# Expert tiles and shared units of a mixture-of-experts layer, interleaved stage by stage on TensorE; the tiles' down part in three fp32r products

## The chip, the cores and the metric

One core of a Trainium2 chip runs the whole program. The metric is the device time of one execution in microseconds; for the kernel before it was taken in three runs, and one more execution was profiled. TensorE is called PE in the profile, VectorE DVE, ScalarE ACT, GpSimd POOL, and SyncE, which issues most DMAs here, SP.

## The reference

A transformer layer on 2048 tokens of width 512, all in fp32: windowed attention, residual and layer norm, then a feed-forward part with a second residual and layer norm. The feed-forward part is

```python
logits = x @ W_router.T
probs = softmax(logits)
rw, sel = top_k(probs, 2)                                  # 8 experts, 2 per token
combine = zeros((T, 8)).at[arange(T)[:, None], sel].add(rw)
sh = silu_and_mul(x @ Ws_gate_up, 1408) @ Ws_down          # shared expert
shared_out = sh * sigmoid(x @ W_sgate.T)
h = silu_and_mul(einsum('th,ehi->eti', x, We_gate_up), 352)
eo = einsum('eti,eih->eth', h, We_down)
sparse_out = einsum('eth,te->th', eo, combine)
x = layernorm(x + shared_out + sparse_out)
```

## The kernel before

The attention half is the same in both kernels and ends at about 430 us of the profile. What follows is `ffn_phase`.

Nearly every product there is made of three fp32r passes: an operand a is split into a_hi (a copy rounded to fp32r, by ScalarE) and a_lo = a - a_hi (by VectorE), and TensorE accumulates a_lo b_hi, a_hi b_lo and a_hi b_hi.

*Units.* The shared expert has 1408 hidden columns, worked off in 11 units of 128 for each of four runs of 512 tokens, 44 units in all. A unit n has a gate part, an up part and a down part, each of twelve passes of 512 columns. ScalarE applies SiLU to the gate sum, VectorE multiplies it with the up sum (`work`), both split the result into `h_hi` and `h_lo`, and the down part of unit n stands behind the gate and up parts of unit n + 1. Weights come through rings of three buffers. Gate and up sums have two PSUM banks each, the down sums four.

*Routing.* A router product, then VectorE finds the top two experts of each token, counts tokens per expert and gives each pair of token and expert a slot in 39 tiles of 128 rows. One-hot tables (`onehot_rows`, `onehot_lanes`, L1091 to L1101) and 32 small fp32 products (`index_tokens`, L1264, recorded as 64) turn this into a list of tokens per tile. The one-hot tables are made after unit 6 and TensorE uses them ahead of unit 8 (`PREFIX_AT, INDEX_AT = 4, 8`).

*Tiles.* After the first 11 units all 39 tiles follow without a unit between them. For tile i GpSimd gathers 128 rows of x; TensorE transposes them (`transpose_xe`, L1312); gate and up are 24 passes of 352 columns (`expert_gate_up`, L1322); VectorE multiplies into `e_h`; TensorE transposes h (`transpose_h`, L1338), ScalarE copies it out of PSUM; and the down part (`expert_down`, L1344) is three products in plain fp32, each recorded as two passes of 512 columns. Its result goes to DRAM (`expert_rows`). The expert's weights, 704 KB twice and 512 and 192 KB, are loaded anew for each tile; only gate and up weights are split, into the buffers that the units use, so that no unit can be under way. The tile's steps alternate between two PSUM banks of each kind.

*Combine.* Units 11 to 43 follow. Between them GpSimd gathers for each block of 128 tokens the two expert rows (`gather`), VectorE adds them with their weights (`add_rows`, two operations), adds the shared sum (`evacuate`), takes the statistics, and normalises (`normalise`), with the reciprocal root from GpSimd (`rstd_of`). This is spread over all three later runs of tokens.

The order on each engine is written out by hand as loops; each engine works its queue in that order and waits on semaphores. SP issues the loads in its own loop, each behind the wait that frees its buffer.

## Time and profile before

| | us |
|---|---|
| median of 3 runs | 1146.53 |
| lowest, highest | 1141.86, 1148.76 |
| the profiled execution | 1145.41 |
| its span, from the first to the last instruction | 1143.6 |

Share of the span that each engine was busy: PE 94%, weight loads (PEld) 75%, DVE 62%, ACT 49%, POOL 34%. The DMA queues moved 175.78 MB. A share of busy time is a mean over stages with different limits, so the rows further down go by stage. A matmul's record is longer than the distance to the next one, so distances between starts, not durations, give the pace. "issue" means that the engine waited for nothing that the profile shows.

### The profile page before, as it was taken

The numbers are of one execution on the slowest core, as the hardware profiler recorded it, in microseconds if no ns is written. First come the engines' busy times: TensorE is split into PE (matmuls) and PEld (weight loads), VectorE is DVE, ScalarE is ACT, GpSimd is POOL, SyncE is SP. The second block draws the span as 40 slices with busy tenths as digits, with TensorE's granted clock in tenths as the row PEclk, the third lists the DMA queues.
The fourth block names the chain that finished last, engine by engine and source line by source line (L and its number), as shares of the span: only waits on it lengthen the run. The fifth ranks groups of instructions, "written<-read, shape, count | busy, mean of one in ns | idle before, by whom it ended". The sixth has DMA issues, their size and how long they took to land.

```text
span 1143.6 us, 19457 instructions
## 1 busy us (share of the span) xinstructions
PE 1078.9 (94%) x7063; PEld 857.4 (75%) x7063; DVE 706.9 (62%) x1100; ACT 560.9 (49%) x1191; POOL 387.0 (34%) x529
## 2 busy tenths in 40 slices
PE   4799999999999968999999999999999999999995
PEld 3577777777777748888777777777777888878884
DVE  4697878777778741565465555565554575465465
ACT  3566666666666531332356666666663243332330
POOL 2777887687787720000001111110102221012012
PEclk8899999999999985898999999999999999999998
DMA  5102111111111005132589999999987474175132
GB/s 195 30 24 57 30 31 30 42 48 31 30 31 48 20 19 165 56 111 74 200 294 355 358 364 366 365 362 368 359 287 221 129 243 125 46 225 169 58 111 74
DMA packets 123678, 175.78 MB, mean 154 GB/s; under 512 B 10592, under 2 KB 64224, under 8 KB 123584
## 3 DMA queue, kind: packets, MB, share of 16 engines
q1 hardware_dynamic: 117904, 155.92, 41.8%
q0 software_dynamic: 5680, 18.62, 5.1%
q8 instruction: 57, 0.93, 0.4%
q14 instruction: 37, 0.30, 0.1%
HBM read 155.90 MB, written 18.61 MB: 153 GB/s over the span
## 4 chain that ended last, share of the span: by engine, by line
PE 55%; DVE 4%; DMA 1%; issue 1%; ACT 1%; SPq 0%; POOLq 0%; POOL 0%; DVEq 0%; ACTq 0%
PE down_ps L1352 9%; PE gate_ps L1292 3%; PE gate_ps L1294 3%; PE gate_ps L1293 3%; PE up_ps L1294 3%; PE up_ps L1292 3%; PE up_ps L1293 3%; PE down_ps L1308 3%; PE down_ps L1310 3%; PE down_ps L1309 3%; PE gate_ps L1333 3%; PE up_ps L1251 2%; PE gate_ps L1334 2%; PE gate_ps L1335 2%; PE up_ps L1333 2%; PE up_ps L1335 2%
## 5 line engine op out<-in xcount | busy, mean ns | idle before, releaser
L864 POOL DMA_INDIRECT rows<-x_dram,token_i x39 | 37.8, 970 | 362.0 <-PE gate_ps L1319 254.8
L1165 DVE TENSOR_TENSOR gu_lo<-e_raw,gu_hi 128x1408 fp32r<-128x1408 f32 x78 | 126.6, 1623 | 50.3 <-ACT gu_hi L935 50.0
L310 ACT ACTIVATE prob<-score_ps,nbias 128x256 f32<-128x256 f32 x256 | 119.6, 476 | 9.2 <-DVE nbias L407 8.8
L935 ACT CAST gu_hi<-e_raw 128x1408 fp32r<-128x1408 f32 x78 | 106.6, 1367 | 29.1 <-DMA e_raw<-in_We_gu 26.9
L247 POOL TENSOR_TENSOR probT<-probT,masks 128x256 f32<-128x256 f32 x128 | 97.2, 780 | 66.2 <-DVE probT L428 66.1
L1352 PE MATMUL down_ps<-ed_raw,y 128*128 128x512 f32 (+1 forms) x234 | 106.9, 593 | 0.6 <-ACT y L955 0.6
L1113 DVE TENSOR_TENSOR work<-work,up_ps 128x512 f32<-128x512 f32 x44 | 30.2, 687 | 117.3 <-PE up_ps L1294 113.1
L496 PE MATMUL proj_ps<-wqkv_lo,xT_hi 128*128 128x512 f32 x192 | 86.4, 450 | 15.7 <-DVE wqkv_lo L385 9.9
L407 DVE TENSOR_REDUCE nbias<-score_ps 128x2 f32<-128x512 f32 x128 | 88.5, 691 | 4.4
L915 ACT ACTIVATE work<-gate_ps 128x512 f32<-128x512 f32 x44 | 26.3, 598 | 120.0 <-PE gate_ps L1294 119.8
L318 ACT COPY probT<-probT_ps 128x512 f32<-128x512 f32 x64 | 37.5, 587 | 92.8 <-PE probT_ps L530 92.8
L497 PE MATMUL proj_ps<-wqkv_hi,xT_hi 128*128 128x512 f32 x192 | 78.5, 409 | 0.0
L498 PE MATMUL proj_ps<-wqkv_hi,xT_lo 128*128 128x512 f32 x192 | 78.2, 407 | 0.0
L1352 PEld LDWEIGHTS down_ps<-ed_raw,y 128*128 128x128 f32 (+1 forms) x234 | 43.3, 190 | 38.1 <-issue 37.3
L1292 PE MATMUL gate_ps<-x_hi,gu_lo 128*128 128x512 f32 x176 | 71.1, 404 | 0.4 <-DVE gu_lo L1014 0.4
L530 PE MATMUL probT_ps<-ident,prob 128*128 128x128 f32 x512 | 71.3, 283 | 0.0
L1293 PE MATMUL gate_ps<-x_lo,gu_hi 128*128 128x512 f32 x176 | 70.2, 399 | 0.0
L1294 PE MATMUL gate_ps<-x_hi,gu_hi 128*128 128x512 f32 x176 | 70.2, 399 | 0.0
L875 POOL DMA_INDIRECT rows<-expert_rows,slot_i x32 | 34.5, 1078 | 104.1 <-DVE y L1141 59.0
L1308 PE MATMUL down_ps<-wd_hi,h_lo 128*128 128x512 f32 x176 | 68.8, 391 | 0.7 <-DVE h_lo L1117 0.7
L1169 DVE TENSOR_TENSOR h_lo<-gate_ps,h_hi 128x512 fp32r<-128x512 f32 x39 | 27.0, 691 | 68.1 <-ACT h_hi L943 68.1
L1292 PE MATMUL up_ps<-x_hi,gu_lo 128*128 128x512 f32 x176 | 68.7, 390 | 0.0
...
## 6 DMA issues: line engine op xcount, KB each, us to landing
...
```

Of the source, the lines that this page charges most:

```text
L247: nc.gpsimd.tensor_tensor(probT[:, heads, 2, :], probT[:, heads, 0, :], own_T.unsqueeze(1).to_broadcast([P, 2, P]), ALU.mult).then_inc(own ...
L310: nc.scalar.activation(prob[:, g % 2, h, :], score_ps[:, h, 0:2 * P], ACT.Exp, bias=nbias[:, s % 2, head:head + 1], scale=1.0, accum_out=r ...
L407: nc.vector.tensor_reduce(nbias[:, s % 2, at:at + 2], score_ps[:, heads, 0:2 * P], mybir.AxisListType.X, ALU.max, negate=True).then_inc(ma ...
L496: nc.tensor.matmul(out, l_hi[:, k, :], w_lo[:, k, cols], start=(k == 0), stop=False)
L497: nc.tensor.matmul(out, l_hi[:, k, :], w_hi[:, k, cols], start=False, stop=False)
L935: nc.scalar.copy(e_hi[:, part, :], src).then_inc(e_hi_made, 1)
L1165: nc.vector.tensor_tensor(e_lo[:, part, :], src, e_hi[:, part, :].bitcast(FP32), ALU.subtract).then_inc(e_lo_made, 1)
L1292: nc.tensor.matmul(o, gu_lo[:, n % RING3, k, part], x_hi[:, tt % 2, k, :], start=(k == 0), stop=False)
L1293: nc.tensor.matmul(o, gu_hi[:, n % RING3, k, part], x_lo[:, tt % 2, k, :], start=False, stop=False)
L1294: last = nc.tensor.matmul(o, gu_hi[:, n % RING3, k, part], x_hi[:, tt % 2, k, :], start=False, stop=(k == KT - 1))
L1308: nc.tensor.matmul(down_ps[i][:, :], hl, wd_hi[:, n % RING3, :], start=(u == 0), stop=False)
L1352: last = nc.tensor.matmul(down_ps[i % 2][:, :], e_hT[0:DN[u], i % 2, u * P:(u + 1) * P], ed_raw[0:DN[u], i % 2, u * H:(u + 1) * H], start= ...
```

## The change

All engines now follow one list, `ORDER`. It holds the stages gate n, up n, down n - 1 of every unit, and behind each such stage, from unit 7 on, one stage of the tiles: `turn` i (the transpositions of tile i's h and of tile i + 1's x) or `expert` i (tile i's down part, then gate and up of tile i + 1). So two unit stages stand in each tile's time, and the 39 tiles reach to unit 32. The first tile's x is transposed, and its gate and up made, right behind unit 5's down part.

For this the tiles get their own buffers and PSUM banks: units have one gate and one up bank, tiles one each. The rings of split weights shrink from three to two, x's residual is read into the space of the transposed x. The tiles' down weights and h are split too, and the down part is nine fp32r passes. Routing moves up (`PREFIX_AT` 3, `INDEX_AT` 6). The combine of all blocks moves into units 34 to 41, two blocks per unit, and is dealt out anew: ScalarE scales the gathered rows, GpSimd adds the two, VectorE adds the sum, GpSimd makes a third small operation per block, and ScalarE normalises.

```diff
-    PREFIX_AT, INDEX_AT = 4, 8
+    RAW, HALVES = 3, 3
+    PREFIX_AT, INDEX_AT, FIRST_TILE_AT, COMBINE_AT = 3, 6, 7, 34
...
+    def order():
+
+        stages, waiting = [], []
+        for n in range(NU):
+            for kind, m in (("gate", n), ("up", n), ("down", n - 1)):
+                if m >= 0:
+                    stages.append((kind, m))
+                if n == FIRST_TILE_AT - 1 and kind == "down":
+                    stages += [("turn", -1), ("expert", -1)]
+                    waiting = [(stage, i) for i in range(TILES) for stage in ("turn", "expert")]
+                elif waiting:
+                    stages.append(waiting.pop(0))
+        return stages + waiting + [("down", NU - 1)]
+
+    ORDER = order()
...
-        gate_ps = [bank(f"gate_ps{i}") for i in range(2)]
-        up_ps = [bank(f"up_ps{i}") for i in range(2)]
+        gate_ps, up_ps, e_gate_ps, e_up_ps = bank("gate_ps"), bank("up_ps"), bank("e_gate_ps"), bank("e_up_ps")
...
+                if stage == "gate" and n == INDEX_AT:
+                    sp.wait_ge(routed, 2)
+                    next_expert(0)
+                    next_expert(1)
+                    for i, half in ((0, 0), (0, 1), (1, 0)):
+                        load_expert(i, half)
+                    load_expert_down(0)
+                if stage == "turn" and n + 2 < TILES:
+                    load_expert(n + 2, 1)
+                if stage == "expert":
+                    if n >= 0:
+                        store_rows(n)
+                    next_expert(n + 3)
+                    if n + 3 < TILES:
+                        load_expert(n + 3, 0)
+                    if n + 2 < TILES:
+                        load_expert_down(n + 2)
...
+            def sum_rows(b):
+
+                pool.wait_ge(rows_scaled, 2 * (b + 1))
+                nc.gpsimd.tensor_tensor(gathered(b, 0), gathered(b, 0), gathered(b, 1), ALU.add).then_inc(rows_summed, 1)
...
+                pool.wait_ge(y_rstd, b + 1)
+                nc.gpsimd.tensor_scalar(rstd[:, b % 2, 2:3], mv[:, b % 2, 0:1], rstd[:, b % 2, 0:1], -1.0, ALU.mult, ALU.mult).then_inc(y_shift, 1)
+
+            for b in range(4):
+                gather(b)
+            for b in range(0, NB, 2):
+                sum_rows(b)
+                sum_rows(b + 1)
+                for c in (b + 4, b + 5):
+                    if c < NB:
+                        gather(c)
+                for c in (b, b + 1):
+                    if c < NB - BT:
+                        rstd_of(c)
+            for b in range(NB - BT, NB):
+                rstd_of(b)
...
+            def scale_rows(b):
+                act.wait_ge(rows_loaded[b % 4], 32 * (b // 4 + 1))
+                for t in range(TOP_K):
+                    nc.scalar.activation(gathered(b, t), gathered(b, t), ACT.Identity, scale=top[:, b, t:t + 1]).then_inc(rows_scaled, 1)
+
+            def normalise(b):
+                act.wait_ge(y_shift, b + 1)
+                nc.scalar.activation(y_block(b), y_block(b), ACT.Identity, bias=rstd[:, b % 2, 2:3], scale=rstd[:, b % 2, 0:1]).then_inc(y_normed, 1)
...
+            for stage, n in ORDER:
+                if stage == "gate":
+                    act.wait_ge(gate_mm, n + 1)
+                    if n:
+                        act.wait_ge(h_made, n)
+                    nc.scalar.activation(silu[:, :], gate_ps[:, :], ACT.Silu).then_inc(silu_made, 1)
+                    for b in range(2 * (n - COMBINE_AT), 2 * (n - COMBINE_AT + 1)):
+                        if 0 <= b < NB:
+                            scale_rows(b)
+                if stage == "up":
+                    if n + 2 < NU:
+                        split_gu(n + 2)
+                    split_hidden(n)
+                if stage == "down":
+                    if n + 2 < NU:
+                        split_wd(n + 2)
+                    if 4 <= n % UN < 4 + KT and n // UN + 1 < NT:
+                        split_x(n // UN + 1, n % UN - 4)
+                    for b in range(2 * (n - COMBINE_AT), 2 * (n - COMBINE_AT + 1)):
+                        if 0 <= b < NB - BT:
+                            normalise(b)
+                if stage == "turn":
+                    if n >= 0:
+                        split_hT(n)
+                    if n + 1 < TILES:
+                        split_xe(n + 1)
+                        if n < 0:
+                            split_expert(0, 0)
+                        split_expert(n + 1, 1)
+                if stage == "expert":
+                    if n >= 0:
+                        copy_row(n)
+                    if n + 1 < TILES:
+                        split_expert_down(n + 1)
+                        silu_expert(n + 1)
+                    if n + 2 < TILES:
+                        split_expert(n + 2, 0)
...
-                    dve.wait_ge(y_loaded[b // BT % 2], 16 * (b // BT // 2 + 1))
-                nc.vector.scalar_tensor_tensor(y_block(b), rows[:, 2 * (b % 2), :], top_w(b, 0), y_block(b), ALU.mult, ALU.add).then_inc(row0_added, 1)
-                dve.wait_ge(row0_added, b + 1)
-                nc.vector.scalar_tensor_tensor(y_block(b), rows[:, 2 * (b % 2) + 1, :], top_w(b, 1), y_block(b), ALU.mult, ALU.add).then_inc(rows_added, 1)
-
-            def top_w(b, t):
-
-                return top[:, b, t:t + 1]
+                    dve.wait_ge(y_loaded[NT - 1], 16)
+                nc.vector.tensor_tensor(y_block(b), y_block(b), gathered(b, 0), ALU.add).then_inc(rows_added, 1)
...
+                nc.vector.tensor_tensor(ed_lo[:, 0:DK - 1, :], src[:, 0:DK - 1, :], ed_hi[:, 0:DK - 1, :].bitcast(FP32), ALU.subtract).then_inc(ed_lo_made, 1)
+                last = slice(0, DN[-1])
+                nc.vector.tensor_tensor(ed_lo[last, DK - 1, :], src[last, DK - 1, :], ed_hi[last, DK - 1, :].bitcast(FP32), ALU.subtract).then_inc(ed_lo_made, 1)
...
+                if stage == "up":
+                    multiply(n)
+                    if n + 2 < NU:
+                        split_gu(n + 2)
+                    split_hidden(n)
+                    if n == 0:
+                        router_top()
+                    if n == 1:
+                        router_hits()
+                    if n == PREFIX_AT:
+                        take_before()
+                        place_experts()
+                    if n == PREFIX_AT + 1:
+                        place_tokens()
+                    if n == PREFIX_AT + 2:
+                        onehot_rows()
+                        onehot_lanes()
+                    for b in range(2 * (n - COMBINE_AT), 2 * (n - COMBINE_AT + 1)):
+                        if 0 <= b < NB:
+                            add_rows(b)
+                        if 0 <= b < NB - BT:
+                            statistics(b)
+                if stage == "down":
+                    if n + 2 < NU:
+                        split_wd(n + 2)
+                    if 4 <= n % UN < 4 + KT and n // UN + 1 < NT:
+                        split_x(n // UN + 1, n % UN - 4)
+                    if n % UN == UN - 1 and n < NU - 1:
...
+                if stage == "turn":
+                    if n >= 0:
+                        lower_hT(n)
+                    if n + 1 < TILES:
+                        lower_xe(n + 1)
+                        if n < 0:
+                            lower_expert(0, 0)
+                        lower_expert(n + 1, 1)
+                if stage == "expert":
+                    if n + 1 < TILES:
+                        lower_expert_down(n + 1)
+                        multiply_expert(n + 1)
+                    if n + 2 < TILES:
+                        lower_expert(n + 2, 0)
...
             def expert_down(i):
-                pe.wait_ge(hT_made, i + 1)
-                pe.wait_ge(ed_loaded[i % 2], 32 * (i // 2 + 1))
-                if i >= 2:
-                    pe.wait_ge(row_made, i - 1)
+                pe.wait_ge(hT_lo_made, i + 1)
+                pe.wait_ge(ed_lo_made, 2 * (i + 1))
+                for u in range(DK):
+                    hh, hl = (t[0:DN[u], u * P:(u + 1) * P] for t in (eT_hi, eT_lo))
+                    dh, dl = ed_hi[0:DN[u], u, :], ed_lo[0:DN[u], u, :]
+                    nc.tensor.matmul(e_up_ps[:, :], hl, dh, start=(u == 0), stop=False)
+                    nc.tensor.matmul(e_up_ps[:, :], hh, dl, start=False, stop=False)
+                    last = nc.tensor.matmul(e_up_ps[:, :], hh, dh, start=False, stop=(u == DK - 1))
+                last.then_inc(ed_mm, 1)
...
+            def expert_gate_up(i):
+                pe.wait_ge(xe_lo_made, i + 1)
+                expert_part(i, e_gate_ps[:, 0:I_MOE], slice(0, I_MOE), e_gate_mm)
+                if i:
+                    pe.wait_ge(row_made, i)
                 else:
-                    pe.wait_ge(evacuated, BT)
-                for u in range(DK):
-                    last = nc.tensor.matmul(down_ps[i % 2][:, :], e_hT[0:DN[u], i % 2, u * P:(u + 1) * P], ed_raw[0:DN[u], i % 2, u * H:(u + 1) * H],
-                                            start=(u == 0), stop=(u == DK - 1))
-                last.then_inc(ed_mm, 1)
+                    pe.wait_ge(routed, 2)
+                expert_part(i, e_up_ps[:, 0:I_MOE], slice(I_MOE, GU), e_up_mm)
...
+            for stage, n in ORDER:
+                if stage == "gate":
+                    if n == PREFIX_AT:
+                        count_before()
+                    if n == INDEX_AT:
+                        index_tokens()
+                    gate(n)
+                if stage == "up":
+                    up(n)
+                if stage == "down":
+                    down(n)
+                if stage == "turn":
+                    if n >= 0:
+                        transpose_h(n)
+                    if n + 1 < TILES:
+                        transpose_xe(n + 1)
+                if stage == "expert":
+                    if n >= 0:
+                        expert_down(n)
+                    if n + 1 < TILES:
+                        expert_gate_up(n + 1)
```

On TensorE, in the tiles: at the end of one tile's gate and up, before.

```order
L1335 MATMUL up_ps0<-gu_hi,h_hi 128x352
L1352 MATMUL down_ps0<-ed_raw,y 128x512 [waits row_made,ed_loaded0,hT_made]
L1352 MATMUL down_ps0<-ed_raw,y 128x512 x2
L1333 MATMUL gate_ps1<-gu_lo,h_hi 128x352 [waits hT_made,e_lo_made,xe_lo_made]
L1334 MATMUL gate_ps1<-gu_hi,h_lo 128x352
```

And now, from the transpositions to the next tile's gate.

```order
L1341 MATMUL e_up_ps<-tables,e_h 128x128 x2
L1351 MATMUL e_gate_ps<-tables,rows 128x128 [waits e_silu_made,xe_loaded1]
L1351 MATMUL e_gate_ps<-tables,rows 128x128 x3
L1309 MATMUL gate_ps<-x_hi,gu_lo 128x512 [waits x_lo_made,silu_made,gu_lo_made]
...
L1311 MATMUL gate_ps<-x_hi,gu_hi 128x512
L1360 MATMUL e_up_ps<-ed_hi,eT_lo 128x512 [waits ed_lo_made,hT_lo_made]
L1361 MATMUL e_up_ps<-ed_lo,eT_hi 128x512
L1362 MATMUL e_up_ps<-ed_hi,eT_hi 128x512
...
L1369 MATMUL e_gate_ps<-e_lo,xe_hi 128x352 [waits e_lo_made,xe_lo_made]
```

A unit stage has come between the transpositions and the down part, and the down part waits for split operands. On VectorE, where the one-hot tables are made: before they stand behind a whole unit's work, and one more unit follows before the index is taken.

```order
L1018 TENSOR_TENSOR wd_lo<-wd_raw,wd_hi 128x512 [waits wd_hi_made]
L1010 TENSOR_TENSOR x_lo<-x1T,x_hi 128x512 [waits x_hi_made]
L1092 TENSOR_TENSOR ed_raw<-row_of,tables 128x1248
L1096 TENSOR_TENSOR ed_raw<-ed_raw,tables 128x624 [waits route]
L1096 TENSOR_TENSOR ed_raw<-ed_raw,tables 128x624
L1100 TENSOR_TENSOR e_raw<-lane_of,tables 128x4096 [waits route]
L1113 TENSOR_TENSOR work<-work,up_ps1 128x512 [waits h_lo_made,silu_made,up_mm]
```

Now:

```order
L1164 TENSOR_TENSOR h_lo<-hidden,h_hi 128x512 [waits h_hi_made]
L1140 TENSOR_TENSOR ed_raw<-row_of,tables 128x1248
L1144 TENSOR_TENSOR ed_raw<-ed_raw,tables 128x624 [waits route]
L1144 TENSOR_TENSOR ed_raw<-ed_raw,tables 128x624
L1148 TENSOR_TENSOR e_raw<-lane_of,tables 128x4096 [waits route]
L1066 TENSOR_TENSOR wd_lo<-wd_raw,wd_hi 128x512 [waits wd_hi_made]
L1058 TENSOR_TENSOR x_lo<-x1T,x_hi 128x512 [waits x_hi_made]
L1153 CAST token_i<-e_up_ps 128x39 [waits index_mm]
```

The index is taken directly behind the tables, with no unit's multiplication between. On GpSimd, in the combine, before: the gathers of a run of tokens in one piece, then the small operations.

```order
L875 DMA rows<-expert_rows,slot_i 128x512 x8
L880 TENSOR_SCALAR rstd_y<-mv_y 128x1
L882 TENSOR_TENSOR rstd_y<-rstd_y,half_y 128x1
L880 TENSOR_SCALAR rstd_y<-mv_y 128x1
L882 TENSOR_TENSOR rstd_y<-rstd_y,half_y 128x1
```

Now a round for two blocks, one round per unit:

```order
L900 TENSOR_TENSOR rows<-rows 128x512 x2
L895 DMA rows<-expert_rows,slot_i 128x512 x4
L905 TENSOR_SCALAR rstd_y<-mv_y 128x1
L907 TENSOR_TENSOR rstd_y<-rstd_y,half_y 128x1
L909 TENSOR_SCALAR rstd_y<-mv_y,rstd_y 128x1
L905 TENSOR_SCALAR rstd_y<-mv_y 128x1
L907 TENSOR_TENSOR rstd_y<-rstd_y,half_y 128x1
L909 TENSOR_SCALAR rstd_y<-mv_y,rstd_y 128x1
```

Two sums of 512 columns and one more small operation per block have joined the queue, and the sum of the next round stands behind all of them.

## Rows read from the trace of the kernel before

**Rows 1.** Busy time by stretch: PE, PEld, DVE, ACT, POOL; PEclk, DMA share, GB/s.
```profile
460.00:566.00 106.00, 105.41 (x468) 88.36 (x469) 57.42 (x135) 32.02 (x48) 3.83 (x3) 0.93 0.34 104
575.00:860.00 285.00, 281.91 (x1417) 219.26 (x1418) 164.74 (x154) 175.99 (x228) 33.07 (x35) 0.99 1.00 346
856.00:1134.00 278.00, 273.25 (x1198) 224.32 (x1197) 153.08 (x225) 93.19 (x142) 47.11 (x60) 1.00 0.47 141
```

**Rows 2.** Waits of PE from 430 us: us in total, times, longest.
```profile
PE gate_ps L1333 <- issue: 4.8, 7, 2.5
...
PE gate_ps L1333 <- DVE h_lo L1169: 1.5, 1, 1.5
...
PE down_ps L1308 <- DVE h_lo L1117: 0.7, 1, 0.7
...
PE up_ps L1269 <- DVE e_raw L1100: 0.6, 1, 0.6
```

**Rows 3.** Timeline of PE: start, us; first matmul of two successive units.
```profile
510.80 0.39 PE L1292 MATMUL gate_ps<-x_hi,gu_lo 128*128 128x512 f32 x1
...
518.96 0.39 PE L1292 MATMUL gate_ps<-x_hi,gu_lo 128*128 128x512 f32 x1
```

**Rows 4.** Chain of waits, tile stage: start, us, what.
```profile
574.97 0.63 PE gate_ps L1333
...
578.95 0.44 PE gate_ps L1319 x4
...
586.13 0.44 PE gate_ps L1319 x4
...
588.48 2.58 PE down_ps L1352 x6
...
593.31 0.44 PE gate_ps L1319 x4
...
844.49 0.44 PE gate_ps L1319 x4
```

**Rows 5.** Chain of waits, around the index matmuls.
```profile
519.07 1.38 DVE ed_raw L1092
...
520.47 1.54 DVE ed_raw L1096 x2
...
522.03 4.43 DVE e_raw L1100
...
526.51 10.32 PE up_ps L1269 x64
```

**Rows 6.** Busy time by stretch, PE alone: PE, PEclk, DMA share, GB/s.
```profile
532.00:534.00 2.00, 2.00 (x11) 0.50 0.70 200
```

**Rows 7.** Timeline of POOL, and its groups by shape: busy, mean ns.
```profile
871.60 0.95 POOL L875 DMA_INDIRECT rows<-expert_rows,slot_i  x1 [0.30 <-issue]
...
872.85 0.95 POOL L875 DMA_INDIRECT rows<-expert_rows,slot_i  x1 [0.30 <-issue]
...
L182 POOL TENSOR_TENSOR qk<-rot_a,rot_b 128x512 f32<-128x512 f32 x31 | 39.7, 1279 | 2.4
...
L882 POOL TENSOR_TENSOR rstd_y<-rstd_y,half_y 128x1 f32<-128x1 f32 x16 | 8.9, 554 | 1.3
```

**Rows 8.** Two lines of DVE: duration ns min/median/max.
```profile
L455 DVE TENSOR_TENSOR oT_lo<-oT,oT_hi x16: 692/1182/1233, 71.1 to 419.0; 128x512 fp32r<-128x512 f32 x16
...
L444 DVE TENSOR_TENSOR oT<-oT_ps,oT x16: 690/692/693, 66.7 to 417.7; 128x512 f32<-128x512 f32 x16
```

**Rows 9.** Groups by shape, DVE from 460 us, ACT: busy, mean ns, idle.
```profile
L1165 DVE TENSOR_TENSOR gu_lo<-e_raw,gu_hi 128x1408 fp32r<-128x1408 f32 x78 | 126.6, 1623 | 50.3 <-ACT gu_hi L935 50.0
...
L1014 DVE TENSOR_TENSOR gu_lo<-raw_ring,gu_hi 128x1024 fp32r<-128x1024 f32 x28 | 34.2, 1221 | 20.3 <-ACT gu_hi L903 20.3
...
L935 ACT CAST gu_hi<-e_raw 128x1408 fp32r<-128x1408 f32 x78 | 106.6, 1367 | 29.1 <-DMA e_raw<-in_We_gu 26.9 <-PE up_ps L1335 1.7
...
L921 ACT CAST h_hi<-work 128x512 fp32r<-128x512 f32 x44 | 27.3, 620 | 71.8 <-DVE work L1113 71.7
...
L903 ACT CAST gu_hi<-raw_ring 128x1024 fp32r<-128x1024 f32 x29 | 30.3, 1044 | 35.7 <-DMA raw_ring<-in_Ws_gu 35.6
```

554 lines of the change are left out of this document (204 added, 350 removed).

## The prediction

> **What bounds the kernel now.** I read the table by stretches first: the attention half ends at about 430 us and the change does not touch it; the feed-forward half has a stage of shared units, a stage of expert tiles, and a second stage of units. In all three TensorE is busy for 98 to 99% of the stretch, and in the tile stage the DMA engines are at their full share too, at 346 GB/s [rows 1]. The list of waits confirms it: over 700 us TensorE stands still for a handful of microseconds [rows 2]. So the time is the sum of TensorE's work plus its gaps, and I price the change in those two coins.
>
> The paces come from start-to-start distances, since records of matmuls overlap. A unit of 36 matmuls takes 518.96 - 510.80 = 8.16 us, so 0.227 us per fp32r matmul of 512 columns and 2.72 us per stage (gate, up or down) of twelve [rows 3]. A tile takes at best 593.31 - 586.13 = 7.18 us; the 12 matmuls of 352 columns between a transposition and the next down part take 588.48 - 586.13 - 0.44 = 1.91 us, 0.16 each; the six fp32 passes of the down part take 2.58 us [rows 4]. From tile to tile the mean is (844.49 - 586.13) / 35 = 7.38 us, so 0.20 us a tile is spent waiting for data.
>
> **What the change takes away.**
> Down part: nine fp32r passes at 0.227 are 2.04 us in place of 2.58, so 39 x 0.54 = -21.1 us. The bounds are 0 (if a pass kept the fp32 pace of 0.43) and this; I take this, because the unit's down part has the very form (128 by 512, three products, a new stationary tile for each) and runs at 0.227.
> Waiting for data in the tile stage: 35 x 0.20 = -7.1 us. A tile moves 346 GB/s x 7.38 us = 2.55 MB, and two unit stages add about two thirds of a unit's three 256 KB loads, 0.5 MB; the new period of a tile with its two unit stages is 7.18 - 0.54 + 2 x 2.72 = 12.1 us, so the stage asks for 255 GB/s where 346 were reached. The loads are then covered; if a wait stays, it will be on ScalarE or VectorE.
> The entry into the tile stage: waits of 1.5 and 2.5 us [rows 2], and the slow start after them: from 574.97 to 578.95 stand twelve matmuls and three transpositions worth 2.25 us, so 1.7 us more [rows 4]. Together -5.7 us. The later wait of a unit's down part, -0.7 us [rows 2].
> Sum of the gains: -34.6 us.
>
> **What the change adds.**
> *The index.* The one-hot tables are now built after unit 5 and TensorE wants them only one down stage (2.72 us) later, where before a whole gate-up followed. On VectorE stand in front: the conversion of the next weights (1.04 us on ScalarE, then 1.22), one of 512 columns (0.69, 0.6 in a chain) [rows 8, 9], then the tables, from 519.07 to 522.03 + 4.43 = 7.4 us [rows 5]: 10.4 us with the hand-overs. 10.4 - 2.7 - 0.6 (the present wait [rows 2]) = +7.1 us. No other work stands behind this wait on TensorE's queue that could go first.
> *Its clock.* The 64 short passes take 10.32 us now, and the granted clock is 0.50 in their second half, the lower of its two levels, 1.2 GHz [rows 5, 6]. After a stand of 7.7 us they will run at 0.50 from the first. With about 0.2 us per pass at half and 0.1 at full clock, 25 of the 64 are fast today: +2.5, and a little for the gate behind them; I take +3.0 (bounds 0 and 4).
> *The first tile.* It stands directly behind unit 5's down part, and ScalarE reaches its conversions only then: behind the transposition it converts x in 0.62 and half the weights in 1.37, and VectorE subtracts in 1.62 [rows 9]: 3.6, with hand-overs 3.8 us of waiting, and I add 0.8 for the other half of the weights: +4.6, and again a slow start of 1.7: +6.3 us. Loads and gather have the 8.16 us of unit 6 to land, at a time when nothing else is loaded.
> *The turns.* Between a tile's transpositions (seven, 0.77 us by the 0.44 for four [rows 4]) and its down part lies one unit stage, 3.49 us in all. Where the stage before was an up stage, ScalarE must still convert weights, 1.04 (VectorE multiplies meanwhile), and VectorE subtract 1.22, subtract h, 0.6, and then subtract the transposed h of 384 columns, about 0.55: 3.4, with hand-overs 3.65 us [rows 8, 9]. So 0.2 us at every third turn, 13 x 0.2 = 2.6, and about 1 us at each of the two places where four sums of PSUM (0.69 each, [rows 8]) stand in that queue: +4.4 us. At the other two kinds of turn the margin is 0.9 to 1.7 us, and nothing is charged. VectorE's load in the stage: 165 us of now [rows 1], 39 x (1.22 + 0.69 + 0.55) = 96 us new, and 26 units at 3.6 (1.22 and three or four operations at 0.69): 355 of 39 x 12.1 = 471 us, 75%. It covers, but in a queue with fixed order.
> *The combine.* All sixteen blocks are now combined in units 34 to 41, two per unit. GpSimd's queue per unit: four gathers at 1.25 apart, two sums of 512 columns at 1.28, and six small operations at 0.55 [rows 7]: 5.0 + 2.6 + 3.3 = 10.9 us, against 8.16 of TensorE. Behind a late sum VectorE waits, and behind that the next unit's multiplication, for which TensorE's up stage waits. The first pair can be ready 4.4 us after gate 34 (an activation of 512 columns 0.6, two for the scaling 1.25 [rows 9], sums 2.6) and is needed at 14.0 at the latest, so 9.5 us are covered; six rounds have gathers and statistics: 6 x 2.7 - 9.5 = +6.7 us. Bounds: 0 (if gathers overlap the rest) and 16.2.
> *The two engines' meeting.* In the attention half a VectorE subtraction with both inputs in SBUF takes 0.692 at best and 1.182 in the median beside GpSimd work, while one of the same size that reads PSUM stays at 0.692 [rows 8]. The new addition of rows has both inputs in SBUF and is released just when GpSimd begins the second sum; the gather two places on waits for it. That is a 0.69 us addition in the loop of each round, 6 x 0.69 = +4.1 us (bounds 0 and 8).
> The Trainium skill's page "SBUF — State Buffer", section "Who interferes with whom", says just that: the two share a port pair, and whichever comes second blocks for the whole of the other's instruction. By the rule the price is this 4.1 us, without it 0; the trace agrees by the 1.182.
> The end: VectorE loses its normalisations of the last blocks, GpSimd has one small operation more each and ScalarE the scaling; within 1 us either way, taken as 0. ScalarE's new activation kinds bring no further table load in the program's order.
> Sum of the costs: 7.1 + 3.0 + 6.3 + 4.4 + 6.7 + 4.1 = +31.6 us.
>
> **The sum.** 1143.6 - 34.6 + 31.6 = 1140.6 us of span; the profiled execution's own time, 1145.41, lies 1.8 us above its span, which gives 1142.4. The median of the three runs, 1146.53, lies 1.1 above that execution, within their scatter of 7 us, and I do not add it. I say 1142.5: the tile stage wins 35 us and the two ends of the interleaving give nearly all of it back. One per cent, 11.5 us, is about what a measurement of this kernel can tell from no change.
>
> **Rivals.**
> 1. *The combine is covered.* If gathers cost their queue less than 1.25 us, and sums do not meet VectorE's, the last two terms go (-10.8) and with the clock held at the index another -3.0: 1129 us. For it: GpSimd spans are rough, and the 9.5 us of cover are near what is needed. Against: the 1.25 us spacing is steady. 0.28.
> 2. *The combine becomes the bound, slower.* If each of the four gathers and two sums of a round meets a VectorE operation with two SBUF inputs and is held 0.49 us (1.182 - 0.692), the round is 13.8 us, and 6 x 5.6 - 9.5 = 24.3 us are lost instead of 10.8: 1156 us. It decides from a round of about 11.9 us, beyond which the kernel is slower than before; for it VectorE holds such operations for about 4 us a unit. 0.14, and in half of it over 1158.
> 3. *The turns become the bound.* If VectorE or ScalarE is 0.6 us later than the margins at every turn, 39 x 0.6 = 23 us: 1166 us. For it the 75% load in a fixed order; against, two of three turns have 0.9 us and more to spare. 0.06.
> 4. *The split brings nothing*: if the nine passes wait for their stationary tiles, 21 us are missing: 1163 us. The unit's down part speaks against it. 0.02.
> The forecast itself, 1134 to 1152, has 0.50.
>
> **Range and chances.** From 1126 (rival 1 with its clock and a little more) to 1160 (rival 2 and a part of 3) hold about 8 in 10. Faster by over 1% (under 1135): rival 1 and the forecast's lower edge, 0.32. Slower by over 1%: 0.18. Within: 0.50.
>
> **What would show it.** In the profile after: the nine passes in 2.04 us; a stand of 7 to 8 us before the index matmuls with the granted clock at 0.50 behind it; 4 to 5 us before the first tile's gate; a period of 12.1 us for a tile and two unit stages with the DMA share well under 1; in units 36 to 41 waits of the up matmuls on VectorE's multiplication, with GpSimd busy or issuing without a break and rounds of 11 us. I am wrong if the rounds of the combine are 8.2 us, if the turns show waits on every tile, or if DMA still sits at its full share in the tiles.

## The result and the profile after

The changed kernel takes 1153.31 us in the median of seven runs (1150.23 to 1153.86), the kernel before 1144.61 us on the same chips. The ratio is 1.0071, with a 95% interval of 1.0053 to 1.0089: slower by 0.7%, where I had said 1142.5 us, 0.35% faster than the median shown. It lies inside the range and within 1% of no change, but on the slower side, where I had forecast the faster. The profiled execution has a span of 1152.1 us, 8.5 more than before.

Busy time by engine in the profile after: us, share of the span, number of instructions.

```profile
PE 1067.0 (93%) x7180; PEld 884.4 (77%) x7180; DVE 788.7 (68%) x1185; ACT 645.9 (56%) x1317; POOL 414.7 (36%) x562
```

TensorE is busy for 12 us less than before (1078.9), and the program is 8.5 us longer: TensorE stands still for 85 us instead of 65. I call a stretch in which it waits a stand. The waits of PE after (us in total, times, longest), answering to [rows 2]:

```profile
PE up_ps L1309 <- DVE hidden L1160: 11.3, 5, 2.7
PE e_up_ps L1302 <- DVE e_raw L1148: 7.8, 1, 7.8
PE e_gate_ps L1369 <- DVE e_lo L1195: 4.3, 1, 4.3
...
PE e_up_ps L1360 <- DVE eT_lo L1210: 1.5, 2, 1.1
```

These are the four places that the prediction named, in this order: the combine (five stands), the index, the first tile, the turns. Busy time by stretch (PE, PEld, DVE, ACT, POOL; granted clock, DMA share, GB/s), answering to [rows 1]: the start of the feed-forward half, the tiles with the units between them, the combine.

```profile
430.00:551.00 121.00, 106.57 (x461) 95.21 (x462) 57.13 (x131) 31.89 (x45) 3.61 (x10) 0.75 0.36 109
551.00:1030.00 479.00, 477.25 (x2475) 417.17 (x2475) 343.74 (x390) 302.00 (x420) 37.27 (x36) 1.00 0.80 256
1030.00:1152.00 122.00, 98.08 (x408) 77.81 (x406) 70.22 (x97) 60.33 (x90) 74.05 (x96) 0.94 0.54 168
```

In the tiles the DMA engines run at 0.80 and 256 GB/s (255 were worked out) and TensorE stands for under 2 us in 479. Outside them it stands for 14 us in the first stretch and 24 in the last, of which some 12 are the end that the kernel before has too.

The index and the first tile, in the timeline of PE (start, us, instruction, idle time before and its releaser):

```profile
516.59 13.85 PE L1302 MATMUL e_up_ps<-ed_raw,e_raw 128*128 128x39 f32 x64 [7.82 <-DVE e_raw L1148]
...
541.22 0.60 PE L1351 MATMUL e_gate_ps<-tables,rows 128*128 128x128 f32 x4
546.16 0.62 PE L1369 MATMUL e_gate_ps<-e_lo,xe_hi 128*128 128x352 f32 x1 [4.34 <-DVE e_lo L1195]
547.17 0.49 PE L1369 MATMUL e_gate_ps<-e_lo,xe_hi 128*128 128x352 f32 x1
```

and the granted clock during the index matmuls (PE alone):

```profile
516.60:530.20 13.60, 13.60 (x64) 0.50 0.00 0
```

All 64 run at the lower level, 1.2 GHz, behind the stand of 7.8 us. They take 13.85 us against 10.32 [rows 5], and the gate behind them is slow as well.

One turn behind an up stage, in the same view: a tile's transpositions, a down stage of the shared units, the tile's down part.

```profile
579.20 0.60 PE L1351 MATMUL e_gate_ps<-tables,rows 128*128 128x128 f32 x4
579.55 0.48 PE L1334 MATMUL down_ps<-wd_hi,h_lo 128*128 128x512 f32 x1
579.87 0.40 PE L1335 MATMUL down_ps<-wd_lo,h_hi 128*128 128x512 f32 x1
...
582.14 0.39 PE L1336 MATMUL down_ps<-wd_hi,h_hi 128*128 128x512 f32 x1
582.55 0.50 PE L1360 MATMUL e_up_ps<-ed_hi,eT_lo 128*128 128x512 f32 x1
582.89 0.39 PE L1361 MATMUL e_up_ps<-ed_lo,eT_hi 128*128 128x512 f32 x1
...
584.75 0.33 PE L1369 MATMUL e_gate_ps<-e_lo,xe_hi 128*128 128x352 f32 x1
```

From start to start a matmul of 512 columns takes 0.227 us. The first one behind the transpositions takes 0.32: 0.10 us at every turn. The down part starts 0.41 us behind the last unit matmul, 0.18 late, and its first matmul takes 0.34. The weight load says whom it waited for:

```profile
582.55 0.19 PEld L1360 LDWEIGHTS e_up_ps<-ed_hi,eT_lo 128*128 128x128 f32 x1 [0.44 <-DVE eT_lo L1210]
```

In the combine, GpSimd's queue for one round, its start to the next round's start (timeline of POOL):

```profile
1091.99 2.54 POOL L900 TENSOR_TENSOR rows<-rows 128x512 f32<-128x512 f32 x2
1095.37 1.05 POOL L895 DMA_INDIRECT rows<-expert_rows,slot_i  x1 [0.84 <-DVE x1T L1181]
1096.73 0.95 POOL L895 DMA_INDIRECT rows<-expert_rows,slot_i  x1 [0.30 <-issue]
...
1099.40 1.43 POOL L895 DMA_INDIRECT rows<-expert_rows,slot_i  x1 [0.30 <-issue]
1100.90 0.19 POOL L905 TENSOR_SCALAR rstd_y<-mv_y 128x1 f32<-128x1 f32 x1
...
1103.34 2.55 POOL L900 TENSOR_TENSOR e_raw<-e_raw 128x512 f32<-128x512 f32 x2
```

The round takes 1103.34 - 1091.99 = 11.35 us, a unit 8.16. VectorE's queue in the same stretch:

```profile
1093.31 1.77 DVE L1181 TENSOR_TENSOR x1T<-x1T,rows 128x512 f32<-128x512 f32 x1 [4.04 <-POOL rows L900]
...
1096.01 0.68 DVE L1181 TENSOR_TENSOR x1T<-x1T,rows 128x512 f32<-128x512 f32 x1
```

It stands for 4.04 us before the late sum. Then the addition of rows takes 1.77 us beside GpSimd's second sum, and 0.68 us alone.

TensorE pays more than the waits. From the first matmul of unit 38's gate (1070.56) to the last of the program (1139.66) lie 19 stages of 2.72 us, less one matmul, 51.5 us; it took 69.1, which is 17.6 more. The five stands are 12.1 of it from start to start (11.3 in the list of waits, since a matmul's record is longer than the distance to the next one). The granted clock adds 3.2: it fell behind the second and the fifth stand (2.50 and 2.66 us), where nine matmuls each time take 3.6 us instead of 2.0, and not behind the other three (2.39, 1.29 and 2.47 us). PE alone, behind the second stand, behind the fourth, and in two pieces behind the fifth:

```profile
1087.60:1092.50 4.90, 4.90 (x15) 0.65 0.97 368
1110.30:1115.70 5.40, 5.40 (x24) 1.00 0.55 172
1122.00:1124.00 2.00, 2.00 (x8) 0.76 0.46 131
1124.00:1126.00 2.00, 2.00 (x6) 0.50 0.00 0
```

In the last row 2 us hold six matmuls instead of nine. Another 1.2 us are three short gaps before gates (ahead of 1082.12, 1104.81 and 1116.17). A gate waits for the SiLU of the unit before, since the gate sums have one bank now; and on ScalarE this SiLU stands behind two normalisations, which wait for GpSimd's third small operation:

```profile
1102.14 0.82 ACT L994 ACTIVATE x1T<-x1T,rstd_y 128x512 f32<-128x512 f32 x1 [2.09 <-POOL rstd_y L909]
1103.42 0.82 ACT L994 ACTIVATE x1T<-x1T,rstd_y 128x512 f32<-128x512 f32 x1 [0.45 <-POOL rstd_y L909]
1104.14 0.58 ACT L1010 ACTIVATE silu<-gate_ps 128x512 f32<-128x512 f32 x1
```

The SiLU ends at 1104.72, and the gate's first weight load starts at 1104.78. The first matmul behind each of the eight gaps takes 0.30 to 0.34 us instead of 0.227, 0.8 together, and 0.4 are spread over the others. In the kernel before the same units run without a gap and at 1.00.

### The profile page after: what moved, and what is told of

The parts are those of the page before. It is cut to its first block, busy times and chain, and to the rows that moved or that the text cites. A ratio compares the mean times of both kernels' runs of the same rounds, so it can differ in the third digit from the quotient of the medians.

```text
span 1152.1 us, 20007 instructions
## 1 busy us (share of the span) xinstructions
PE 1067.0 (93%) x7180; PEld 884.4 (77%) x7180; DVE 788.7 (68%) x1185; ACT 645.9 (56%) x1317; POOL 414.7 (36%) x562
## 4 chain that ended last, share of the span: by engine, by line
PE 52%; POOL 4%; DVE 3%; issue 1%; ACT 1%; DMA 0%; POOLq 0%; DVEq 0%; ACTq 0%
PE gate_ps L1309 3%; PE up_ps L1309 3%; PE up_ps L1311 3%; PE up_ps L1310 3%; PE gate_ps L1310 3%; PE gate_ps L1311 3%; PE e_up_ps L1360 3%; PE down_ps L1336 3%; PE down_ps L1335 3%; PE down_ps L1334 3%; PE e_up_ps L1285 2%; PE e_up_ps L1361 2%; PE e_up_ps L1362 2%; PE e_gate_ps L1369 2%; PE e_up_ps L1371 2%; PE e_up_ps L1369 2%
## 5 line engine op out<-in xcount | busy, mean ns | idle before, releaser
L882 POOL DMA_INDIRECT rows<-x_dram,token_i x39 | 40.4, 1035 | 518.0 <-PE e_gate_ps L1351 416.8
L1195 DVE TENSOR_TENSOR e_lo<-e_raw,e_hi 128x1408 fp32r<-128x1408 f32 x78 | 126.6, 1624 | 47.0 <-ACT e_hi L953 47.0
L953 ACT CAST e_hi<-e_raw 128x1408 fp32r<-128x1408 f32 x78 | 107.4, 1379 | 58.6 <-PE e_up_ps L1371 58.6
L1200 DVE TENSOR_TENSOR ed_lo<-ed_raw,ed_hi 128x1024 fp32r<-128x1024 f32 x39 | 47.8, 1226 | 66.5 <-ACT ed_hi L961 66.5
L1309 PE MATMUL up_ps<-x_hi,gu_lo 128*128 128x512 f32 x176 | 71.4, 406 | 11.3 <-DVE hidden L1160 11.3
L1311 PE MATMUL up_ps<-x_hi,gu_hi 128*128 128x512 f32 x176 | 70.3, 399 | 0.0
L1310 PE MATMUL up_ps<-x_lo,gu_hi 128*128 128x512 f32 x176 | 69.9, 397 | 0.0
L399 DVE COPY_PREDICATED score_ps<-masks,score_ps 128x256 f32<-128x256 int32 x128 | 54.0, 422 | 23.1 <-PE score_ps L517 23.0
L1336 PE MATMUL down_ps<-wd_hi,h_hi 128*128 128x512 f32 x176 | 68.9, 391 | 0.0
L1335 PE MATMUL down_ps<-wd_lo,h_hi 128*128 128x512 f32 x176 | 68.8, 391 | 0.0
## 6 DMA issues: line engine op xcount, KB each, us to landing
e_raw<-in_We_gu SPq DMA_DIRECT2D x78, 704.0 KB, 4.6
```

The costliest lines, as they stand in the source:

```text
L953: nc.scalar.copy(e_hi[:, half * HK:(half + 1) * HK, :], raw_half(i, half)).then_inc(e_hi_made, 1)
L1195: nc.vector.tensor_tensor(e_lo[:, part, :], raw_half(i, half), e_hi[:, part, :].bitcast(FP32), ALU.subtract).then_inc(e_lo_made, 1)
L1309: nc.tensor.matmul(o, gu_lo[:, n % 2, k, part], x_hi[:, tt % 2, k, :], start=(k == 0), stop=False)
L1310: nc.tensor.matmul(o, gu_hi[:, n % 2, k, part], x_lo[:, tt % 2, k, :], start=False, stop=False)
L1311: last = nc.tensor.matmul(o, gu_hi[:, n % 2, k, part], x_hi[:, tt % 2, k, :], start=False, stop=(k == KT - 1))
L1335: nc.tensor.matmul(down_ps[i][:, :], hh, wd_lo[:, n % 2, :], start=False, stop=False)
```

## The experiments

Times are medians; the ratio is to the kernel before on the same chip, with its 95% interval. Gains and losses between variants are taken from the spans of the profiled executions. A span has the attention half in it, which no edit touches and which differs by up to 3 us from one execution to another. So the last column counts from the first gate matmul of the shared units (459.59 us in the changed kernel) to the end of the span; the kernel before has 683.6 there.

| run | us | ratio | span | from the first gate |
|---|---|---|---|---|
| changed kernel | 1153.31 | 1.0071 (1.0053 to 1.0089) | 1152.1 | 692.5 |
| a: down part in fp32 again | 1170.1 | 1.0200 (1.0167 to 1.0233) | 1168.7 | 710.0 |
| b: index, tiles, combine one unit later | 1139.34 | 0.9938 (0.9917 to 0.9958) | 1137.7 | 678.4 |
| c: first tile spread | 1150.42 | 1.0046 (1.0029 to 1.0062) | 1148.4 | 689.8 |
| d: sums on VectorE | 1144.16 | 1.0007 (0.9990 to 1.0024) | 1142.3 | 684.8 |
| g: d, stores later | 1135.71 | 0.9929 (0.9902 to 0.9955) | 1133.9 | 675.3 |
| h: stores later alone | 1152.06 | 1.0074 (1.0048 to 1.0101) | 1149.3 | 692.5 |
| e: h split before the weights | 1164.05 | 1.0179 (1.0147 to 1.0212) | 1162.2 | 704.0 |
| i: b, c, g and e | 1139.64 | 0.9954 (0.9935 to 0.9973) | 1138.8 | 680.3 |
| j: b, c and g | 1121.09 | 0.9791 (0.9766 to 0.9817) | 1119.2 | 659.3 |
| k: j, weights split behind the turn | 1117.39 | 0.9760 (0.9734 to 0.9785) | 1116.4 | 656.5 |
| l: kernel before, short down part | 1140.85 | 0.9971 (0.9951 to 0.9991) | 1138.0 | 679.9 |

**a. The split undone.** What the low halves add to the result is left out.

```diff
-                    hh, hl = (t[0:DN[u], u * P:(u + 1) * P] for t in (eT_hi, eT_lo))
-                    dh, dl = ed_hi[0:DN[u], u, :], ed_lo[0:DN[u], u, :]
-                    nc.tensor.matmul(e_up_ps[:, :], hl, dh, start=(u == 0), stop=False)
-                    nc.tensor.matmul(e_up_ps[:, :], hh, dl, start=False, stop=False)
-                    last = nc.tensor.matmul(e_up_ps[:, :], hh, dh, start=False, stop=(u == DK - 1))
+                    hh = eT_hi[0:DN[u], u * P:(u + 1) * P].bitcast(FP32)
+                    dh = ed_hi[0:DN[u], u, :].bitcast(FP32)
+                    last = nc.tensor.matmul(e_up_ps[:, :], hh, dh, start=(u == 0), stop=(u == DK - 1))
```

> The changed kernel with one thing undone: each tile's down part is again three products in plain fp32 (six passes) instead of nine fp32r passes. They read the rounded halves of h and of the weights, so the low halves are made and waited for as before and only TensorE's work differs (what the low halves add to the result is left out). Theory: the split is worth what it was priced at, 39 times 2.58 - 2.06 = 0.52 us, so this kernel is 20 us slower than the changed one (about 1173 us), with the same waits at the index, at the first tile and in the combine. Rival (the split brings little, because the tile stage waits for ScalarE and VectorE anyway): less than 8 us slower, and the turn's waits for the lowered h become shorter by what the passes become longer.

It is 16.6 us slower, 17.5 from the first gate, and all waits are as in the changed kernel (11.2, 7.8, 4.3 and 1.5 us). So the split works: 0.45 us per tile rather than 0.54. From 582.55 to 584.75 and at the other turns the nine passes take 2.06 to 2.20 us. From the first pass to the second matmul of the next gate part it is 2.22 us in the median, with the fp32 form 2.74. That is 0.52 us, nearly what was priced; but 0.07 us come back in the next tile's up part, whose twelve matmuls take 1.97 us in the mean with the split and 1.90 without it. Why is not shown.

**b. Index, first tile and combine one unit later.**

```diff
-    PREFIX_AT, INDEX_AT, FIRST_TILE_AT, COMBINE_AT = 3, 6, 7, 34
+    PREFIX_AT, INDEX_AT, FIRST_TILE_AT, COMBINE_AT = 3, 7, 8, 35
```

> The changed kernel with index, first tile and combine one unit later (INDEX_AT 7, FIRST_TILE_AT 8, COMBINE_AT 35). Theory: TensorE's wait of 7.8 us before the index matmuls goes, since a whole unit (8.16 us) now stands between the tables and their use, and with it the slow clock behind it, of which the changed kernel has 13.65 + 2.8 us against the earlier kernel's 10.1 + 2.0: 4 us more. So 12 us faster than the changed kernel, about 1141 us; the wait of 4.3 us before the first tile and the combine's 11.3 us stay. Rival (the tables are not what is late): under 4 us faster, with the wait moved to another line.

14.4 us faster, the largest single gain, and the wait before the index is gone. The matmuls themselves tell the clock's share:

```profile
516.43 8.76 PE L1302 MATMUL e_up_ps<-ed_raw,e_raw 128*128 128x39 f32 x64
```

8.76 us instead of 13.85 with no stand in front, less even than the 10.32 of the kernel before, which has a stand of 0.6 us there. So of the 14.4 us, 7.8 are the stand and 5.1 the clock on these matmuls; the combine's stands are shorter too (10.2 us instead of 11.3).

**c. One unit stage between the first tile's transposition and its gate.**

```diff
-                    stages += [("turn", -1), ("expert", -1)]
-                    waiting = [(stage, i) for i in range(TILES) for stage in ("turn", "expert")]
+                    stages.append(("turn", -1))
+                    waiting = [("expert", -1)] + [(stage, i) for i in range(TILES) for stage in ("turn", "expert")]
```

> The changed kernel with one unit stage (gate 7, 2.72 us) put between the first tile's transposition and its gate and up. Theory: the 4.3 us before the first tile's gate are ScalarE's and VectorE's conversions (3.6 us) without cover; with 2.72 us of cover about 1.5 us of waiting stay, and part of the slow start behind it (1.6 us) goes: 3 to 4.5 us faster than the changed kernel, about 1149.5 us. Rival (the conversions are held up by ScalarE's and VectorE's other work of the unit, which now comes in between): the wait stays at 4 us, and no gain.

3.7 us faster, 2.7 from the first gate; of the 4.3 us of waiting 1.9 are left, and the combine has six stands of 12.2 us here. One unit stage was not cover enough, as expected.

**d. Weights and sums of the gathered rows on VectorE.**

```diff
-                nc.vector.tensor_tensor(y_block(b), y_block(b), gathered(b, 0), ALU.add).then_inc(rows_added, 1)
+                nc.vector.scalar_tensor_tensor(y_block(b), gathered(b, 0), top[:, b, 0:1], y_block(b), ALU.mult, ALU.add).then_inc(rows_summed, 1)
+                dve.wait_ge(rows_summed, b + 1)
+                nc.vector.scalar_tensor_tensor(y_block(b), gathered(b, 1), top[:, b, 1:2], y_block(b), ALU.mult, ALU.add).then_inc(rows_added, 1)
```

with `scale_rows` (ScalarE) and `sum_rows` (GpSimd) taken out.

> The changed kernel with the gathered rows weighted and added on VectorE, by two operations of 0.75 us per block as in the kernel before; ScalarE's scaling and GpSimd's sums are gone. GpSimd's round falls from 11.35 us to four gathers and six small operations, 5.1 + 3.0 = 8.2 us, as long as a unit. Theory: GpSimd's queue set the pace of units 37 to 42; TensorE's 11.3 us of waits for the multiplication go down to under 1 us, and with them the fall of the granted clock behind each of them (the six rounds took 17.7 us over six units, so 6.4 us are clock): 15 to 17.7 us faster than the changed kernel, 1136 to 1138 us. Rival 1 (only the sums' meeting with VectorE's additions matters, 1.22 us in place of 0.69): 4 us faster. Rival 2 (VectorE becomes the bound: 3.3 us of a unit's own work, four sums at 0.75, two statistics at 0.88 are 8.0 us of 8.16): waits on VectorE stay, with GpSimd idle, and less than 8 us are won.

9.8 us faster, 7.7 from the first gate: far from the theory (15 to 17.7 us), and by its size it would fit rival 2 (less than 8 us, with VectorE as the bound). The run takes out ScalarE's scaling together with GpSimd's sums; in the changed kernel the scaling for the round of 1103.34 ended at 1095.8, so it was not what the sums waited for. The waits for the multiplication are gone, but the down part of two units now waits for the lowered h, 5.2 us together. The chain of waits ahead of the second of them shows that it is not VectorE's sums:

```profile
1092.95 1.42 POOL rstd_y L907
...
1096.12 0.56 POOL rstd_y L907
...
1097.08 0.83 ACT x1T L992
...
1097.93 0.34 SPq L816
...
1098.32 0.43 SPq L57
...
1098.79 4.79 DMA gu_raw<-in_Ws_gu
...
1103.60 1.06 ACT gu_hi L932
...
1104.68 0.55 DVE gu_lo L1057
...
1105.82 0.69 DVE h_lo L1159
```

Read from the top: GpSimd's small operation frees ScalarE's normalisation, that frees the store of the finished block (L816), and only behind that store in SP's queue stands the weight load (L57), which then flies 4.8 us. SP works its queue in order, and its wait for a block that nobody needs held up the weights that TensorE needs.

**g and h. The stores one unit later in SP's queue**, with d (g) and alone (h).

```diff
-                if stage == "gate" and n > COMBINE_AT:
-                    for b in range(2 * (n - COMBINE_AT - 1), min(NB - BT, 2 * (n - COMBINE_AT))):
+                if stage == "gate" and n > COMBINE_AT + 1:
+                    for b in range(2 * (n - COMBINE_AT - 2), min(NB - BT, 2 * (n - COMBINE_AT - 1))):
                         store_out(b)
```

> The kernel with the sums on VectorE, and SP issues the stores of a unit's two finished blocks one unit later in its queue. In the trace of the kernel with the sums on VectorE the chain before the two waits of the down matmuls ran GpSimd's small operations, ScalarE's normalisation, the store's issue on SP, the weight load issued behind it, its 4.8 us of flight, and then the splitting of the weights. Theory: SP's queue was the wait that took the place of GpSimd's; with the stores later the weight loads start on time, TensorE's 5.2 us of waits on h_lo and the slow clock behind them go, and 7 to 8 us are won on that kernel: 1135 to 1137 us, the full 17.7 us off the changed kernel. Rival (VectorE, at some 8 us of work per unit of 8.16, is what is late): the waits stay, and under 2 us are won.

> The changed kernel with the stores one unit later in SP's queue, and nothing else (sums still on GpSimd). Theory: there GpSimd's queue is the bound (rounds of 11.35 us), TensorE waits for VectorE's multiplication behind a late sum and not for weights, so nothing is won: 1152 to 1153 us, waits of 11 us. Rival (SP's queue was the limit in the changed kernel too, and GpSimd only filled the time): 5 us or more faster.

g is 18.2 us below the changed kernel, 17.2 from the first gate, and its PE has no wait over 0.3 us in the combine: from unit 38's gate to the last matmul it takes 52.0 us, so 17.1 of the 17.6 us are back. VectorE is not the bound there, with 72.5 us busy of 100 between 1030 and 1130. h keeps its 11.4 us of waits, and from the first gate it takes 692.5 us like the changed kernel; its span is 2.8 us shorter only because its attention half is. So GpSimd's queue was the bound in the changed kernel, and SP's queue was the next one behind it.

**e. h before the weights.** On ScalarE and VectorE alike:

```diff
                 if stage == "up":
-                    if n + 2 < NU:
-                        split_gu(n + 2)
                     split_hidden(n)
+                    if n + 2 < NU:
+                        split_gu(n + 2)
```

> The changed kernel with the order on ScalarE and VectorE of an up stage turned round: h is split before the weights of unit n + 2, not after. Theory: in every third turn of the tiles (behind an up stage) the down part starts 0.18 us late and its first weight load uncovered 0.13 us more, because the lowered h stands behind 1.05 + 1.22 us of weight splitting. In the tile stage the weights are still in front of the turn's own work, so the queue in front of the lowered transposed h is equally long and nothing is won there unless ScalarE's conversion of h overlaps VectorE's; the sum is 0 to -4 us: 1149 to 1153 us. Rival (the multiplication and ScalarE's hand-over, not the weights, set the start): a later h_lo no longer hides it, and the time stays or rises by up to 2 us.

Neither: 10.1 us slower, 11.5 from the first gate. The turns' waits have grown:

```profile
PE e_up_ps L1360 <- DVE eT_lo L1210: 12.2, 14, 1.1
PE up_ps L1309 <- DVE hidden L1160: 10.4, 5, 2.5
PE e_up_ps L1302 <- DVE e_raw L1148: 9.9, 1, 9.9
```

and the timeline of ScalarE and VectorE at one turn shows how:

```profile
580.13 0.68 DVE L1160 TENSOR_TENSOR hidden<-silu,up_ps 128x512 f32<-128x512 f32 x1
...
580.85 0.62 ACT L946 CAST h_hi<-hidden 128x512 fp32r<-128x512 f32 x1 [2.29 <-DVE hidden L1160]
581.37 1.05 ACT L934 CAST gu_hi<-raw_ring 128x1024 fp32r<-128x1024 f32 x1
581.50 0.69 DVE L1164 TENSOR_TENSOR h_lo<-hidden,h_hi 128x512 fp32r<-128x512 f32 x1 [0.69 <-ACT h_hi L946]
```

ScalarE stands while VectorE multiplies and VectorE stands while ScalarE converts; in the old order the weights fill both gaps. The mistake in my expectation was to count the length of the queue and not its hand-overs.

**j and i. The mends together**, without and with e.

> All the mends together: index, first tile and combine one unit later, one unit stage between the first tile's transposition and its gate, sums on VectorE, stores one unit later, h split before the weights. Theory: the gains add, since each is a stand of TensorE at another place: 14.4 (measured for the later index) + 3.7 (measured for the spread first tile) + 17.7 (the combine's six rounds) + 0 to 4: 36 to 40 us off the changed kernel's 1153.3, 1114 to 1118 us, some 27 us under the kernel before. Rival (they cover one another, or the combine one unit later runs into the end of the program: the last four blocks are gathered in units 41 and 42 of 43): 10 us less, 1125 us or more.

> All the mends but the turned order of h and weights, which alone cost 10 us: index, first tile and combine one unit later, one unit stage between the first tile's transposition and its gate, sums on VectorE, stores one unit later. Theory: the measured gains add, 14.4 (later index) + 3.7 (spread first tile) + 17.6 (sums and stores): 35.7 us off the changed kernel's 1153.3, 1117.5 us, 2.3% under the kernel before, and the 22 us that the kernel with all five mends was above this was the order alone. Rival (the combine one unit later runs into the end, or the mends cover one another): 1125 to 1130 us, with waits in units 41 to 43 or before the end.

j is 32.9 us below the changed kernel by span, 33.3 from the first gate. Counted like that the single gains are 14.1, 2.7 and 17.2, together 34.0: they add. i is 19.6 us above j, 21.0 from the first gate, more than the 11.5 of e alone. Its PE waits 13.8 us at the turns where j has 2.9. Before its index there is again a stand, of 1.8 us, behind which the 64 matmuls take 13.1 us at a granted clock of 0.52, where j has no stand and 8.4 us. And its gates in the combine wait for 2.9 us. So by the traces about 11 us lie in the turns, 6 in the index and 3 in the combine.

**k. The weights split behind the turn**, where a turn follows an up stage.

```diff
+    BEFORE_TURN = {m for (kind, m), after in zip(ORDER, ORDER[1:]) if kind == "up" and after[0] == "turn"}
...
                 if stage == "up":
-                    if n + 2 < NU:
+                    if n + 2 < NU and n not in BEFORE_TURN:
                         split_gu(n + 2)
...
+                    if n in LATE and LATE[n] + 2 < NU:
+                        split_gu(LATE[n] + 2)
                 if stage == "expert":
```

(`LATE` gives the unit that belongs to a turn; the same on both engines.)

> The kernel with the four mends, and on ScalarE and VectorE the splitting of unit n + 2's gate and up weights moved behind the turn wherever a turn follows unit n's up stage (every third turn). Theory: there the lowered transposed h stands behind 1.05 + 1.22 us of weight splitting, and the down part starts 0.18 us late with its weight load uncovered (0.13 us): 13 times 0.31 is 4 us, plus the one place where four down sums follow. The weights have over a unit of slack before gate n + 2. So 3 to 4 us faster than without it, 1113.5 to 1114.5 us. Rival 1 (the hidden sum's own splitting, not the weights, is what is late): no change. Rival 2 (as with h before the weights, ScalarE and VectorE stand idle where the weights filled the time, and the time comes back in the expert stage): 5 us or more slower.

2.8 us faster than j by span, 3.7 by the medians. The turns' share shows in the waits of the weight loads (PEld), of j and of k:

```profile
PEld e_up_ps L1357 <- DVE eT_lo L1207: 9.5, 15, 1.9
```

```profile
PEld e_up_ps L1363 <- DVE eT_lo L1211: 3.4, 2, 1.9
```

Fifteen waits have become two, the ones behind four sums of PSUM. k is the best version: 2.4% faster than the kernel before (0.9760, 0.9734 to 0.9785).

**l. The kernel before with a third of its down part.** What the other two products add is left out.

```diff
-                for u in range(DK):
...
-                                            start=(u == 0), stop=(u == DK - 1))
+                for u in range(1):
...
+                                            start=True, stop=True)
```

> The kernel before, with a tile's down part cut to the first of its three products (two recorded passes of six; what the others add is left out). Loads, splits and order are unchanged. TensorE has 1.7 us less to do per tile, 67 us in all. Theory: the DMA engines are at their full share in that stage (1.00 at 346 GB/s, 2.55 MB per tile), so a tile still takes its 7.3 us, and under 8 us are won: faster fp32r passes alone, without the units between the tiles, would have brought next to nothing, and the interleaving is what makes the split worth 17 us. Rival (the transfers have slack, and TensorE's work sets the pace): 40 to 67 us faster.

5.6 us by span, 3.7 from the first gate, 0.3% by the runs, for 57 us less of busy TensorE between 575 and 860 us alone. In that stage, and for the waits:

```profile
575.00:860.00 285.00, 224.78 (x1273) 191.59 (x1272) 163.30 (x153) 174.75 (x231) 33.15 (x35) 0.99 0.99 344
```

```profile
PE gate_ps L1333 <- issue: 60.0, 38, 2.5
```

What TensorE no longer does it stands for, once per tile, with the DMA engines at 0.99, and a tile still takes 7.3 us. In the old order faster passes were worth next to nothing; between units, where the DMA share is 0.80, they are worth 17.5 us (run a). The interleaving without the split is 2.0% slower than the kernel before (run a again). The two halves of the change need each other.

## Why the prediction was right and wrong

Term by term, in the span; the stages of shared units, 132 of 2.72 us in both kernels, are taken out.

| term | predicted | measured | how |
|---|---|---|---|
| tiles (split, data waits, entry, first tile, turns) | -23.2 | -18.1 | before 563.15 to 868.57 less 4 stages, 294.5; after 541.22 to 1029.76 less 78 stages, 276.4 |
| index and its clock | +10.1 | +11.6 | before 0.8 + 10.1 + 2.0; after 8.0 + 13.7 + 2.8 |
| combine | +10.8 | +17.6 | above |
| late wait of a down part | -0.7 | -1.0 | the wait and the slow matmuls behind it |
| start and end of the half | 0 | -1.6 | first gate 0.4 earlier and 0.4 shorter; end 12.9 to 12.2 |
| sum | -3.0 | +8.5 | |

**The combine is the step that failed**, by 6.8 of the 11.5 us. Its mechanism was as written: GpSimd's round of 11.35 us (10.9 + 0.69 predicted) against a unit's 8.16, late sums, the wait of the up matmuls on the multiplication in the last units. The term was mis-sized: 10.8 us predicted, 17.6 measured. The stands themselves are 1.3 us longer than priced (12.1 from start to start). The rest had no term at all: 3.2 us of granted clock behind two of the five stands, 1.2 us of gates that wait for a late SiLU, and 1.2 us of slower first matmuls and of what is spread over the others. I had priced the clock behind the index and behind the first tile, and left it out where the waits were short and many; and the path from GpSimd's small operations over ScalarE's normalisation and SiLU to the gate I had not seen. Run g, which removes the cause, gives 17.1 of the 17.6 us back, all parts together.

*The two engines' meeting* was there as described, and larger than priced: the first addition of a round takes 1.77 us against 0.68 alone, 1.09 us more where I took 0.69 in all, and GpSimd's gather waits 0.84 us for it. My rounds still come out at about the measured length, which is in part luck: the four gathers took 5.5 us for 5.0, and the six small operations 2.4 for 3.3. The Trainium skill's page "SBUF — State Buffer", section "Who interferes with whom", has the later one of VectorE and GpSimd wait for the other's instruction; the 1.77, which is 0.68 and most of GpSimd's second sum of 1.27 us, agrees. In run d it goes the other way as well: GpSimd's small power operation, 0.56 alone, is recorded at 1.42 us (the first row of that chain) beside VectorE's splitting of weights,

```profile
1092.71 1.24 DVE L1057 TENSOR_TENSOR gu_lo<-raw_ring,gu_hi 128x1024 fp32r<-128x1024 f32 x1 [0.56 <-ACT gu_hi L932]
```

and the two small operations behind it, 0.27 and 0.19 alone, take 0.79 and 0.71 beside VectorE's two sums.

**The tiles** fell short by 5.1 us. The period is (1011.96 - 554.70) / 37 = 12.36 us, where I had 12.08 and 4.4 us for the turns, so some 6 us in 38 periods were not in the sum. The larger part is that a matmul of 512 columns behind a short transposition takes 0.10 us more, 38 times, 3.8 us. The tile of the kernel before has this seam inside its 7.18 us (a matmul of 352 columns takes 0.25 there instead of 0.16); the new tile has it in the unit stage, yet its own parts still take 6.66 us, for 6.64 priced, because of the slower up part of run a. The turns cost 5.8 us instead of 4.4 (twelve at 0.31, one of 1.4 and one of 0.7 where sums of PSUM stand in the queue or the stages end), and the last 1 us lies in the other seams. Against that the kernel before had lost 1.7 us more in its tile stage than I had counted; 0.8 us of the 5.1 are not placed. The nine passes take the 2.04 us that they were priced at, with 0.02 over, but by run a the split as such is worth 17.5 us and not 21.1.

**The index** was right in stand (8.0 less the 0.8 of before, for 7.1) and 1.4 short in clock: 1.0 of it on the 64 matmuls, which had run in 10.1 us before and took 13.6, and 0.3 to 0.4 on the stages behind them. **The first tile** was priced at 6.3 us and cost 4.5 + 1.6 (its gate part takes 3.56 us instead of 1.93). **The data waits** are gone, as foreseen.

**The rivals.** That the combine is covered (0.28) is refuted: the rounds are 11.35 us, and the 9.5 us of cover were used up by unit 38. That it is the bound by far (0.14) is nearer in result, but by another way: not every gather is held up, the rounds are not 13.8 us, and the price grew by what came behind and beside the stands. The turns as the bound (0.06) were not so in the changed kernel, but run e shows how near they are: two operations exchanged on two engines, 11.5 us. That the split brings nothing (0.02) is refuted by run a.

**The chances.** The sum of gains and the sum of costs were both over 30 us, and what was left between them was 3. A forecast of the sign from such a difference has no more worth than the smallest term left out of either sum; "within 1%" was the right place for half of the chance, and the sign should have been left open.
